# Perceiver block on one core: all four compute engines' order rewritten, one slot per tile operation

## The reference

```
x = x + xattn(ctx_1024, layernorm(x), mask, Wq, Wk, Wv, Wo, rel_bias)
x = x + attn(layernorm(x), norm_g, norm_b, Wq, Wkv, q_scale, k_scale, null_kv, Wout)
x = x + ffn(layernorm(x), wi, bi, wo, bo, lora_A, lora_B, gate_w, gate_b)

xattn: 16 heads of 16; q from x, k and v from 256 context rows;
       softmax(q k^T + rel_bias[bucket(j - i)], masked keys -1e9) v, then Wo
attn:  16 heads of 64; q from a second layernorm, k and v from x, 2 learned null keys;
       q and k scaled to unit length per head; softmax(8 q k^T + alibi, causal) v, then Wout
ffn:   8 experts; logits, softmax, top 2; relu(h wi^T + bi + (h A_e^T) B_e^T) wo^T + bo,
       summed over the two chosen experts, each times the sum of the two top scores
```

## Time and profile before

| | us |
|---|---|
| median of 3 runs | 1953.61 |
| lowest and highest | 1949.09 to 1953.96 |
| the profiled execution | 1951.37 |
| its span, first to last instruction | 1949.6 |
| PE busy | 1563.4 (80%) |
| DVE busy | 1455.7 (75%) |
| ACT busy | 1138.2 (58%) |
| POOL busy | 446.0 (23%) |

### The profile page before, as it was taken

How to read it: one execution, slowest core, us unless ns; L and a number is a source line. 1 busy time by engine, 2 the same in 40 slices (tenths; PEclk the granted TensorE clock), 3 DMA queues, 4 the chain that set the end, 5 groups by cost and what they waited for, 6 DMA issues and landing times.

```text
span 1949.6 us, 50419 instructions
## 1 busy us (share of the span) xinstructions
PE 1563.4 (80%) x16771; PEld 1079.8 (55%) x16771; DVE 1455.7 (75%) x4339; ACT 1138.2 (58%) x2961; POOL 446.0 (23%) x556
## 2 busy tenths in 40 slices
PE   2378888888888888888888888888888888888876
PEld 1145555556555655655565655565565556555554
DVE  2667777888777788777787877778877777787763
ACT  2566555666555566655566655556665655665551
POOL 1122221222222122222122222212222211222220
PEclk7589999999999999999999999999999999999997
DMA  8321222012222101222201222220122221022100
GB/s 205 106 60 56 64 63 62 20 42 62 62 62 62 47 20 58 62 62 62 62 26 36 62 62 62 62 58 13 53 62 62 62 62 38 26 60 62 49 4 6
DMA packets 81195, 108.73 MB, mean 56 GB/s; under 512 B 7608, under 2 KB 63492, under 8 KB 81160
## 3 DMA queue, kind: packets, MB, share of 16 engines
...
## 4 chain that ended last, share of the span: by engine, by line
DVE 45%; PE 29%; issue 12%; POOL 5%; DMA 3%; ACT 2%; DVEq 2%; SPq 1%; POOLq 1%; ACTq 0%
DVE S L1130 5%; PE ps_f L444 4%; DVE x_n L1084 3%; PE ps_f L446 3%; PE ps_f L445 3%; DVE a_raw L1195 3%; PE ps_t L526 3%; DVE aS L1215 3%; DVE a_len L1189 2%; DVE a_sum L1231 2%; DVE a_mx L1222 2%; DVE akT L1204 2%; PE ps_o L542 2%; PE ps_a L637 2%; DVE S L1139 2%
## 5 line engine op out<-in xcount | busy, mean ns | idle before, releaser
L526 PE MATMUL ps_t<-ident,S 128*128 128x128 f32 x1024 | 219.4, 300 | 150.6 <-DVE S L1139 118.0
L834 ACT ACTIVATE S<-S,x_nmx 128x256 f32<-128x256 f32 x512 | 258.0, 505 | 47.1 <-DVE x_nmx L1130 41.4
L846 ACT ACTIVATE pT<-ps_t 128x256 f32<-128x256 f32 x512 | 188.1, 373 | 116.9 <-PE ps_t L526 116.0
L1130 DVE CUSTOM_DVE_ANT_0 S<-ps_s,bias 128x256 f32<-128x256 f32 x512 | 214.8, 420 | 34.0 <-PE ps_s L516 30.5
L526 PEld LDWEIGHTS ps_t<-ident,S 128*128 128x128 f32 x1024 | 112.4, 147 | 202.9 <-DVE S L1139 160.5
L1503 POOL TENSOR_TENSOR a_len<-a_len,half 128x16 f32<-128x16 f32 x64 | 193.5, 3024 | 9.0
L1139 DVE TENSOR_SCALAR S<-S,x_inv 128x256 f32<-128x256 f32 x512 | 180.9, 353 | 18.3
L516 PE MATMUL ps_s<-kst,qst 128*128 128x256 f16 x512 | 142.9, 280 | 38.4 <-DVE x_nmx L1130 29.3
L1457 POOL TENSOR_SCALAR x_rs<-x_mv 128x1 f32<-128x1 f32 x32 | 11.6, 363 | 701.8 <-DVE x_mv L1080 701.8
L444 PE MATMUL ps_f<-zT,f_loraB 128*128 128x128 f16 x512 | 104.0, 222 | 2.1 <-ACT f_h L958 2.1
L604 PE MATMUL ps_a<-ident,a_raw 128*128 128x128 f32 x512 | 81.4, 284 | 28.7 <-DVE akT L1204 28.6
...
## 6 DMA issues: line engine op xcount, KB each, us to landing
...
```

Source lines behind the costliest of these rows:

```text
L526: last = turn(ps_t[t % 2][:, c * P:(c + 1) * P], S[:, t % S_BUFS, c * P:(c + 1) * P], ident[:])
L834: go(S[:, t % S_BUFS, :], S[:, t % S_BUFS, :], ACT.Exp, bias=x_nmx[:, t:t + 1], scale=-1.0, accum_out=x_sum[:, t:t + 1]).then_inc(sem["exp ...
L846: go(pT[:, t % PT_BUFS].rearrange("p c m -> p (c m)"), ps_t[t % 2][:, 0:2 * P], ACT.Copy)\
L1130: nc.vector.tensor_tensor_reduce(out=S[:, t % S_BUFS, :], in0=ps_s[t % 2][:, 0:TK], in1=bias[:, pair, :], scale=-1.0, scalar=BIG, op0=ALU. ...
```

## The change

Every number of `SLOT` is new, the sixteen tiles are given slots of their own by name, and `x_merge` gets slots too (before, it stood behind the loop over slots). No operation, shape, buffer, semaphore or wait changes. SP's code is the same. The table cut to some lines, then the loops:

```diff
-SLOTS = range(-14, 2 * (XTILES + TURN_LAG + PV_LAG))
+SLOTS = range(-14, 43)
 SLOT = dict(
-    pe_x_k=(-14, -14), pe_x_out=(-14,), pe_x_v=(-14, -6), pe_x_turn=(-14,), pe_a_out=(-10,), pe_x_q=(-14,),
+    pe_x_scores=(7, 7, 7, 9, 11, 13, 13, 14, 15, 17, 17, 21, 27, 29, 29, 30),
+    dve_x_bias=(-2, -2, 0, 1, 2, 5, 6, 10, 12, 13, 15, 18, 28, 32, 36, 37),
...
@@ PE
-                        t = s // 2
-                        if s % 2 == 0 and 0 <= t < XTILES:
+                        for t in due("pe_x_scores", s):
                             x_scores(i, t)
-                        if s % 2 == 1 and 0 <= t - TURN_LAG < XTILES:
-                            x_turn_probs(i, t - TURN_LAG)
-                        if s % 2 == 1 and 0 <= t - TURN_LAG - PV_LAG and (t - TURN_LAG - PV_LAG) % QUAD == QUAD - 1:
-                            x_pv(i, (t - TURN_LAG - PV_LAG) // QUAD)
+                        for t in due("pe_x_turn_probs", s):
+                            x_turn_probs(i, t)
+                        for n in due("pe_x_pv", s):
+                            x_pv(i, n)
...
@@ DVE
-                        t = s // 2
-                        if s % 2 == 0 and 0 <= t < XTILES:
+                        for t in due("dve_x_bias", s):
                             x_bias(i, t)
-                        if s % 2 == 1 and 0 <= t - 1 < XTILES:
-                            x_scale(i, t - 1)
+                        for t in due("dve_x_scale", s):
+                            x_scale(i, t)
+                        for n in due("dve_x_merge", s):
+                            x_merge(i)
                 if isinstance(i, int) and i == 0:
                     setup()
-                if do_x:
-                    x_merge(i)
```

More of the change, by code:

```diff
@@ new lines @@
+    act_x_copy_k=(-14, -14), act_x_copy_turned=(-14,), act_x_spread_q=(-14,), act_x_copy_v=(-7, -7),
+    act_x_split_ctx=(18,), act_x_exp=(-8, -8, -5, -1, 2, 4, 5, 13, 17, 18, 23, 25, 29, 39, 40, 40),
+    act_x_copy_probs=(-1, 2, 3, 5, 17, 17, 17, 20, 23, 23, 39, 40, 40, 40, 40, 40), act_x_merge=(42,),
+    act_f_copy_turned=(-13,), act_f_exp=(-9,), act_f_copy_z=(-8,), act_f_relu=(1, 19), act_f_split_hid=(23, 38),
+    act_a_copy_turned=(-14, -14), act_a_copy_k=(-13, -13), act_a_copy_q=(-9, -9), act_a_copy_v=(-6, -6),
@@ new lines @@
+    act_a_spread=(4, 12), act_a_exp=(19, 20), act_a_copy_probs=(24, 24, 26, 27), act_a_copy_pv=(40, 40),
+    dve_x_residual=(-13,), dve_x_split_turned=(-14,), dve_x_split_k=(-11, -11), dve_x_spread_q=(-4,),
+    dve_x_stats=(38,), dve_x_norm=(39,), dve_x_bias=(-2, -2, 0, 1, 2, 5, 6, 10, 12, 13, 15, 18, 28, 32, 36, 37),
+    dve_x_merge=(40,), dve_x_scale=(-1, 0, 1, 2, 5, 9, 10, 12, 13, 15, 25, 28, 32, 36, 37, 38),
+    dve_a_residual=(-8,), dve_a_stats=(-12, -9), dve_a_norm=(-10, -5), dve_a_split_turned=(-6, -4),
@@ new lines @@
+    dve_a_lengths=(-3, -2), dve_a_unit=(0, 1), dve_a_place_keys=(2, 4), dve_a_bias=(13, 13, 15, 15),
+    dve_a_softmax_top=(14, 16), dve_a_softmax_end=(16, 18), dve_a_split_pv=(38, 42),
+    dve_f_stats=(-8,), dve_f_norm=(-4,), dve_f_split_turned=(-4,), dve_f_logits=(-3,), dve_f_route=(-2,),
+    dve_f_split_z=(-1,), dve_f_second=(10, 29), dve_f_split_hid=(32, 36), dve_f_final=(40,),
+    pool_f_rstd=(-3,), pool_f_keep=(30,),
+    pool_a_rstd=(-9, -6), pool_a_length=(0, 7), pool_a_keep=(25,),
@@ L91 @@
+    pool_x_keep=(-14,), pool_x_rstd=(21,), pool_x_mask=(14,), pool_x_split_ctx=(7,),
 )
@@ L1029, in step @@
                     if do_x:
-                        t = s // 2
-                        if s % 2 == 0 and 0 <= t < XTILES:
+                        for t in due("act_x_exp", s):
                             x_exp(i, t)
-                        if s % 2 == 1 and 0 <= t - TURN_LAG < XTILES:
-                            x_copy_probs(i, t - TURN_LAG)
-                if do_x:
-                    x_merge(i)
+                        for t in due("act_x_copy_probs", s):
+                            x_copy_probs(i, t)
+                        for n in due("act_x_merge", s):
+                            x_merge(i)
             split_hi(0)
```

23 lines of the change are left out of this document (5 added, 18 removed).

## The result

| | before | change |
|---|---|---|
| median, us | 1953.78 (4 runs) | 1751.29 (4 runs) |
| lowest and highest | 1949.09 to 1954.20 | 1749.69 to 1754.68 |
| profiled execution | 1951.37 | 1749.69 |
| mean round | 57.5 | 50.3 |

The ratio is 0.8971 (95% interval 0.8951 to 0.8991): 202 us less, where 160 were forecast.

The account below looks back on a forecast made before the run. Waits between PE (80% busy) and DVE (75%) bound the kernel. A 19.7, B 30.55 and C 1.7 make a round of 52.0 for 57.5; -160 over 29 rounds, ends +5.4 - 4.5 - 1.3, give 1791 us; range 1750 to 1865.

Parts of the forecast that it names:

- Stretch C: End of the last `x_scale` to the next `x_k`: 6.8 us before, forecast 1.7 with `f_y` off this path.
- the seam: Where B meets C: `x_norm` delayed the last transpose 2.93 us, the clock fell to 0.50 and `f_y` took 5.1 us.
- Stretch A: Round's head, first `x_k` matmul to first `x_bias`: 15.1 us before, forecast 19.7, range 18.6 to 20.2.
- The first path: In A, DVE up to `x_spread_q`, then q's DMAs: first scores at 19.4 at the latest, first `x_bias` at 19.7.
- the second path: In A, DVE's own queue ahead of `x_bias`, from `f_norm` through the router to the second `a_lengths`: ends at 18.5.
- the rival named better: q's DMAs land before DVE is ready (A 18.6), POOL's split meets one-input operations (B 29.3): 1723 us; chance 0.08.
- Stretch B: First `x_bias` to end of the last `x_scale`, limited by DVE: 35.9 us before, forecast 30.55.
- POOL's block: In B, POOL's split of the context blocks the subtraction in `a_softmax_top` on DVE: 1.25 us, bounds 0 to 2.1.
- The rival built on the rule: POOL's power blocks DVE's `f_route` and `a_unit`, some 4.5 us per round: 1924 us; chance 0.02.
- Step 0: Run's start: the chain of eight weight pieces is delayed by an `x_exp` and an `x_scale`: +5.4 us, 0 to 8.
- ACT late: Rival: ACT's copies come in groups and DVE waits for `x_exp`, 3 us per round: 1880 us; chance 0.10.
- The clock's fall at `f_y`: Rival: the clock falls before `f_y` and returns as it ends, +2.2 us per round: 1857 us; chance 0.15.

Follow-up runs that it names:

- e3: The change with `f_y` alone put back behind the last transpose on TensorE; 1855.49 us, ratio 0.9501.
- e7: The kernel before with 13 unused matmuls put into TensorE's pause ahead of the last transpose; 1900.01 us, ratio 0.9722.
- e5: The kernel before with `x_norm` late, second `f_split_hid` and `f_y` early, `f_final`, `x_turn`, `x_q`, `x_out` and POOL's context split moved; 1870.56 us.
- e8: The change with its seam put back: `x_norm`, POOL's context split, `f_y` and second `f_split_hid`; new head and tile order stay; 1983.20 us, ratio 1.0152.
- e10: e6 with VectorE's setup left behind `x_merge` as in the change; 1740.25 us, ratio 0.8905.
- e6: The change with step 0's late weight splits hung on tiles as before and VectorE's setup ahead of `x_merge`; 1736.34 us, ratio 0.8889.

## Why the prediction was right, and where its terms were off

**Luck in the total.** The rounds alone came out 48 us better than laid out. Without the 6.7 us by which the ends came out worse the time would have been below 1750, outside the range. That it is inside is luck; the mechanism is not.

**Stretch C and the seam.** Right, and the largest part: C 1.98 for 1.7, clock 1.00, `x_norm` 0.46. The reason given for the clock was incomplete. It was that the fall had followed a pause of 2.93 us and that no pause of the new order was above 1.8 us. e3 has no pause above 1.64 us and the clock falls all the same, in 23 of 29 rounds. What keeps it up in every round of the change is `f_y`'s own place among the last tiles, which the prediction counted only as cover. e7 confirms the other half: fill the pause, and the clock stays.

**Stretch A.** 18.86 for 19.7. The first path, with the DMAs for q, was said to decide. It did not. The first of these rows ends at 1027.31, 9.95 us into the round (10.05 forecast):

```profile
1026.46 0.85 DVE L1111 SCALAR_TENSOR_TENSOR qT<-ps_f,qT 64x256 f16<-64x256 f32 x2
...
1029.26 1.24 SPq L324 DMA_DIRECT2D qst<-q_hbm  x2
...
1035.42 0.38 PE L672 MATMUL ps_f<-ident,zr 128*128 128x128 f32 x2
1035.64 0.38 PE L516 MATMUL ps_s<-kst,qst 128*128 128x256 f16 x2
```

The loads of q were issued by 1030.5 and take 4.6 us to landing (median of the page), so q was there by 1035.1 at the latest; the term was 9.3 and is at most 7.8. The store of q landed in 1.8 us (median), where it was 2.8 before, beside k's. The first scores follow at once on the router's transpose (line 672), which waits for DVE, and the first `x_bias` (1036.22) on the second `a_lengths` of DVE's own queue (1034.94, 1.21 us): the second path, forecast at 18.5, decides, as in the rival named better. Its two bare waits came out as laid out, 1.34 us for f's transposed copy (1.2) and 0.50 for `f_z` (0.5).

**Stretch B.** 29.46 for 30.55. The sum ahead of the two new terms was 28.55. POOL's block cost 0.66 in place of 1.25: the mechanism was right and the cost within its bounds (0 to 2.1), but the subtraction that was to be blocked began first, and the victim was an `x_scale`. In e5, where POOL began first, the same subtraction took 1.53 us, +0.82. What remains of the other waits is 29.46 - 28.55 - 0.66 = 0.25, where 0.75 was taken. DVE is idle 1.3 us of B (28.13 busy of 29.46), where under 1 us was forecast.

The Trainium skill, SBUF — State Buffer, section "SBUF: two separate sides", says that whichever of the two starts first holds the shared port pair for its whole instruction. In the main this case's traces agree for the split of the context in both directions (the subtraction first: it keeps 0.71 us and POOL takes 2.33; POOL first: 1.01 us for `x_scale`, 2.21 for `x_norm`, each ending 0.15 us after POOL). A full block of POOL until the subtraction's end would have cost it 0.34 us; it took 0.21 more than its 2.12. For POOL's power they do not, again:

```profile
1036.71 2.94 POOL L1500 TENSOR_TENSOR a_len<-a_len,half 128x16 f32<-128x16 f32 x1
...
1037.80 1.22 DVE L1193 TENSOR_TENSOR a_raw<-a_raw,a_len 128x1024 f32<-128x1024 f32 x1
```

`a_unit`, with two SBUF inputs, runs wholly inside the power in its usual 1.22 us. The rival built on the rule (1924) did not come.

**Round.** 50.3 for 52.0: 1.7 a round, 48 us in all, which is more than the whole difference between forecast and result (41). The parts: A 0.8, B 1.1, C -0.3.

**The router moved into the head.** The prediction booked it as 5.5 us out of B against 4.6 into A. e8 shows what head and tiles are worth with the old seam: A +3.7, B -3.7 and C +0.6, that is nothing.

**Ends.** Step 0 was the worst term: +5.4, bounds 0 to 8, measured +10.4. The named cause, weight splits ahead of an `x_exp`, was right in kind (e10), but it was counted for one tile. DVE waited twice (6.59 and 8.59 us), and the delay began sooner: ACT's split of the second late piece, `a_wk`, starts at 54.41 where it was 48.99, and that of the last at 85.21 where it was 78.17. The setup chain behind `x_merge` was not in the sum, 4 us by e6 against e10. Step 1 was to gain 4.5 and gained nothing; its granted clock is 0.82 (0.85 before), and why it gains nothing was not tried. The end gained 4.2 where 1.3 was taken. Ends together: +6.3 for -0.4.

**Rivals.** ACT late did not come: DVE waited in the rounds hardly at all for `x_exp`. The clock's fall at `f_y` (1857) did not come in the change. e3's 1855 is no measure of it, since there `f_y` is on the path as well; but it shows that the clock falls in most rounds once `f_y` stands five slots later. Slower than before: that a round of this new order can be slower than the old one is shown by e8 (1983), by the seam and not by the fall over the round's turn (clock 1.00 in A).
